# A mixture-of-experts layer whose expert blocks get fixed widths by rank of size, with weights loaded in 512 KB pieces

## What is computed

```python
logits = xf @ router_w
probs = jax.nn.softmax(logits, axis=-1)
topw, topi = jax.lax.top_k(probs, K)                    # K = 2 of E = 8 experts
h = jax.nn.silu(jnp.einsum('nd,edf->nef', xf, w1))      # w1: 8 x 1024 x 1024
ye = jnp.einsum('nef,efd->ned', h, w2)                  # w2: 8 x 1024 x 1024
routed = jnp.einsum('ne,ned->nd', combine, ye)
shared = jax.nn.silu(gate) * up @ shared_down
shared = jax.nn.sigmoid(xf @ shared_gate_w) * shared
return (routed + shared).reshape(b, t, d)
```

## Time and profile before

| | us |
|---|---|
| median of 3 executions | 1111.06 (1108.30 to 1111.72) |
| profiled execution, first to last instruction | 1107.2 |
| TensorE busy with matmuls | 1091.6 |
| DVE busy | 640.2 |
| ACT busy | 482.5 |
| POOL busy | 68.5 |
| share of 16 DMA engines, weights' queue | 33.4% |

### The profile page before, as it was taken

How to read it: one execution, slowest core, us unless ns; L and a number is a source line. 1 busy time by engine, 2 the same in 40 slices (tenths; PEclk the granted TensorE clock), 3 DMA queues, 4 the chain that set the end, 5 groups by cost and what they waited for, 6 DMA issues and landing times.

```text
span 1107.2 us, 16462 instructions
## 1 busy us (share of the span) xinstructions
PE 1091.6 (99%) x6240; PEld 949.3 (86%) x6240; DVE 640.2 (58%) x883; ACT 482.5 (44%) x713; POOL 68.5 (6%) x88
## 2 busy tenths in 40 slices
PE   7999999999999999999999999999999999999998
PEld 5889998787788999878789999898888988988877
DVE  6789967765666753343474423355655646555546
ACT  4503344557786221301324222245655646556540
POOL 2000000000000000000000530200000000000003
PEclk9999999999999999999999999999999999999999
DMA  7222201213322203622004442567577585666648
GB/s 251 76 77 77 76 11 67 76 58 124 104 77 77 71 13 126 207 77 76 1 1 170 152 111 77 169 256 254 190 255 261 184 292 205 241 234 226 235 153 283
DMA packets 76188, 157.02 MB, mean 142 GB/s; under 512 B 7130, under 2 KB 7628, under 8 KB 76131
## 3 DMA queue, kind: packets, MB, share of 16 engines
q1 hardware_dynamic: 64600, 127.30, 33.4%
q10 hardware_dynamic: 7306, 15.41, 3.8%
q0 software_dynamic: 4224, 13.55, 3.8%
HBM read 135.69 MB, written 20.54 MB: 141 GB/s over the span
## 4 chain that ended last, share of the span: by engine, by line
PE 89%; DVE 3%; ACT 2%; DMA 2%; DVEq 1%; issue 1%; POOL 1%; POOLq 0%; SPq 0%; ACTq 0%
PE ps L1725 21%; PE ps L1727 21%; PE ps L1726 21%; PE ps L2146 10%; PE ps L2147 5%; PE ps L1817 1%; PE ps L1764 1%; PE ps L2049 1%; PE ps L2050 1%; PE ps L1980 1%; PE ps L1981 1%; PE ps L1831 1%; DMA y_second<-expert_rows,slots 1%; ACT src_oh L808 1%; ACT w_hi L694 1%
## 5 line engine op out<-in xcount | busy, mean ns | idle before, releaser
L1025 DVE TENSOR_TENSOR w_lo<-w_raw,w_hi 128x2048 fp32r<-128x2048 f32 x107 | 242.3, 2290 | 135.7 <-ACT w_hi L694 133.4
L694 ACT CAST w_hi<-w_raw 128x2048 fp32r<-128x2048 f32 x107 | 201.5, 1911 | 86.4 <-PE ps L2050 36.2
L2146 PE MATMUL ps<-xe,w_hi 128*128 128x448 f32 x512 | 160.9, 375 | 0.0
L2147 PE MATMUL ps<-xe,w_lo 128*128 128x224 f32 x512 | 134.8, 263 | 0.0
L2146 PEld LDWEIGHTS ps<-xe,w_hi 128*128 128x128 f32 x512 | 95.9, 187 | 7.9
L1725 PE MATMUL ps<-w_hi,he_hi 128*128 128x512 f32 (+1 forms) x256 | 101.2, 395 | 0.0
L1727 PE MATMUL ps<-w_hi,he_lo 128*128 128x512 f32 (+1 forms) x256 | 100.2, 391 | 0.0
L1726 PE MATMUL ps<-w_lo,he_hi 128*128 128x512 f32 (+1 forms) x256 | 100.0, 391 | 0.0
L1725 PE MATMUL ps<-w_hi,xt_hi 128*128 128x512 f32 (+1 forms) x240 | 96.0, 400 | 4.0 <-DVEq L1334 2.0
L2147 PEld LDWEIGHTS ps<-xe,w_lo 128*128 128x128 f32 x512 | 97.5, 190 | 0.4
L1727 PE MATMUL ps<-w_hi,xt_lo 128*128 128x512 f32 (+1 forms) x240 | 93.7, 390 | 0.0
(11 more groups left out here) (330 smaller groups left out, 2001.0 us busy)
## 6 DMA issues: line engine op xcount, KB each, us to landing
w_raw<-in_L_ffn_w SPq DMA_DIRECT2D x64, 1024.0 KB, 5.6
w_raw<-in_L_gnn_W_neigh SPq DMA_DIRECT2D x8, 1024.0 KB, 5.5
w_raw<-in_L_gnn_W_self SPq DMA_DIRECT2D x8, 1024.0 KB, 5.1
w_raw<-in_L_ffn_shared_gate_up SPq DMA_DIRECT2D x8, 1024.0 KB, 6.3
w_raw<-in_L_mix_Wv SPq DMA_DIRECT2D x4, 1024.0 KB, 5.7
w_raw<-in_L_mix_Wk SPq DMA_DIRECT2D x4, 1024.0 KB, 5.0
w_raw<-in_L_mix_Wq SPq DMA_DIRECT2D x4, 1024.0 KB, 4.9
w_raw<-in_L_mix_Wo SPq DMA_DIRECT2D x4, 1024.0 KB, 5.0
```

What stands on the lines that cost most here:

```text
L694: copy(w_hi[b][:, s * HK:(s + 1) * HK, :], w_raw[s][:, :, :]).then_inc(hi_done, 1)
L1025: V_.tensor_tensor(w_lo[b][:, k, :], w_raw[s][:, :, :], as32(w_hi[b][:, k, :]), ALU.subtract).then_inc(lo_done, 1)
L2146: mat(PS(key)[:, a, 0:2 * B], wh[:, k, w_cols], xe[:, :, k, 0:B], start=k == 0, stop=False)
L2147: last = mat(PS(key)[:, a, 0:B], wl[:, k, w_cols], xe_hi[:, k, 0:B], start=False, stop=k == KF - 1)
```

## The change

- The experts are ranked by their number of rows on the chip (some 20 more small DVE instructions in the routing stage). Seven blocks have a fixed width (`CAPS`): ranks 2 and 3 get 208 rows, ranks 4 to 6 get 152, ranks 7 and 8 get 128. They are written out, not looped, in the order of ranks 2, 8, 3, 7, 4, 5, 6 (`ORDER` counts from rank 2 as 1), that is 208, 128, 208, 128, 152, 152, 152. A block of 128 has a single row tile; one of 152 has tiles of 128 and 24, one of 208 of 128 and 80.
- The loop of 224-row blocks stays behind them. It serves the largest expert (rank 1) and the rows of any expert that pass its fixed width. With the counts above no expert passes its width (203 and 201 of 208; 149, 147, 145 of 152; 121 and 71 of 128), and the loop runs once.
- Weights of the experts come in four pieces of 512 KB for each job (`PARTS`). SP reloads, ACT casts, DVE subtracts and TensorE waits piece by piece (`weights_in`).
- The zeros for all slots behind the fixed ones, 2016 rows or 8.3 MB, are written by POOL's queue at the start of the kernel from `ctx_s`, in 16 transfers; the zeros ahead of the loop (5.5 MB) are gone.
- POOL reads the token numbers of the twelve fixed tiles into `cols_f` with twelve transfers besides the two for the loop, all ahead of the first gather.

```diff
-    MAXB = X + (2 * N - X) // B + 1
-    SLOTS = MAXB * B
-    SLOTC = SLOTS // 112
-    assert SLOTC * 112 == SLOTS
+    CAPS = (208, 208, 152, 152, 152, 128, 128)
+    ORDER = (1, 7, 2, 6, 3, 4, 5)
+    FIXED = len(ORDER)
+    assert sorted(ORDER) == list(range(1, X)) and len(CAPS) == FIXED and max(CAPS) <= B
+    CAP = [CAPS[r - 1] for r in ORDER]
+    ROWS_OF = [(128, c - 128) if c > 128 else (c,) for c in CAP] + [BROWS]
+    TILE_AT = [sum(len(rows) for rows in ROWS_OF[:q]) for q in range(FIXED + 1)]
+    FIRST_ROW = [sum(CAP[:q]) for q in range(FIXED + 1)]
+    STATIC = FIRST_ROW[FIXED]
+    by_cap = sorted(CAPS)
+    MAXB = 1 + max(m + (2 * N - sum(by_cap[:m - 1]) - m) // B for m in range(1, X + 1))
+    SLOTS = STATIC + MAXB * B
+    SLOTC = -(-SLOTS // 112)
...
-    units += [("sd", 0, 0)] + [("xe", s, f) for s in range(BC) for f in range(2)]
+    xe_units = lambda q: [("xe", q, s, f) for s in range(len(ROWS_OF[q])) for f in range(2)]
+    y_units = lambda q: [("y", q, h, s) for h in range(2) for s in range(len(ROWS_OF[q]))]
+    he_units = lambda q: [("he", q, n) for n in range(KF // 2)]
+    units += [("sd", 0, 0)] + xe_units(0)
     units += [("sd", 0, i) for i in range(1, NT)]
+    for q in range(FIXED):
+        units += he_units(q) + xe_units(q + 1)[:2] + y_units(q)[:1] + xe_units(q + 1)[2:] + y_units(q)[1:]
     U0 = len(units)
...
+    PARTS = 4
...
+            every = sp.value_load(table[0:1, 1, 1:2], min_val=X, max_val=FIXED + MAXB - 1)
+            sp.wait_ge(lo_done, count_at(J_D, 1))
+            with sp.Fori(0, every) as j:
                 expert = sp.value_load(table[0:1, 0, bass.ds(j, 1)], min_val=0, max_val=X - 1)
                 for i in range(4):
                 for i in range(4):
-                    for s in range(2):
-                        sp.wait_ge(lo_done, j * 8 + (2 * (J_X + i - 1) + s + 1))
-                        view = (w1v if i < 2 else w2v)[:, bass.ds(expert, 1), s * HK:(s + 1) * HK,
+                    for s in range(PARTS):
+                        sp.wait_ge(lo_done, j * (4 * PARTS) + (count_at(J_X + i, s) - PARTS))
+                        view = (w1v if i < 2 else w2v)[:, bass.ds(expert, 1), s * PK:(s + 1) * PK,
                                                        (i % 2) * HW:(i % 2 + 1) * HW]
-                        sp.dma_start(w_raw[s][:, :, :], view.rearrange("p e k n -> p (e k) n")).then_inc(w_loaded[s], 16)
...
+            pool.wait_ge(pads_set, 1)
+            for r, count in ZEROED:
+                pool.dma_start(y_d[r:r + count, :], ctx_s[0:count, :, :].rearrange("p n t -> p (n t)")).then_inc(y_zeroed, 16)
...
+            for q in range(FIXED):
+                for s, rows in enumerate(ROWS_OF[q]):
+                    t, r = TILE_AT[q] + s, FIRST_ROW[q] + s * 128
+                    pool.dma_start(cols_f[0:rows, t:t + 1], slot_d[r:r + rows, :]).then_inc(cols_loaded, 16)
...
-            pool.wait_ge(ready[slot(("up", KF - 1))], use(("up", KF - 1)) + 1)
-            pool.wait_ge(prod_done, KF)
-            nc.gpsimd.memset(zrow[:, :], 0.0)
...
+            for q in range(1, FIXED):
+                pool.wait_ge(lo_out, rows_in[q - 1])
+                gather_rows(q)
...
+                if job >= J_X:
+                    for s in range(PARTS):
+                        act.wait_ge(part_loaded[s], by(16 * (job - J_X + 1), base, 64))
+                        copy(w_hi[b][:, s * PK:(s + 1) * PK, :], raw_part(s)).then_inc(hi_done, 1)
+                    return
...
+            def expert(q, j=None):
+
+                job, width = J_X + 4 * q, sum(ROWS_OF[q])
+                for h in range(2):
+                    split_hi(job + h + 1, j)
+                    for n in range(h * HK // 2, (h + 1) * HK // 2):
+                        key = ("he", q, n)
+                        in_s = he_s[:, n % 2, :, 0:width]
+                        wait_unit(key, j)
+                        copy(in_s, PS(key)[:, :, width:2 * width]).then_inc(he_copied, 1)
+                        act.wait_ge(he_added, by(q * (KF // 2) + n + 1, j, KF // 2))
+                        nc.scalar.activation(in_s, in_s, ACT.Silu).then_inc(silu_done, 1)
+                        act.wait_ge(silu_done, by(q * (KF // 2) + n + 1, j, KF // 2))
+                        copy(he_hi[:, 2 * n:2 * n + 2, 0:width], in_s).then_inc(hi_out, 1)
...
+            for q in range(FIXED):
+                expert(q)
...
-            act.wait_ge(zrow_set, 1)
-            for s in range(BC):
-
-                act.dma_start(y_b[block_rows(s), MAXB - 1, 0:HW], zrow[0:BROWS[s], 0:HW]).then_inc(y_stored[s], 16)
-                act.dma_start(y_b[block_rows(s), MAXB - 1, HW:D], zrow[0:BROWS[s], HW:D]).then_inc(y_rows, 16)
-            with act.Fori(blocks, MAXB - 1) as j:
-                for s in range(BC):
-                    act.dma_start(y_block(j, s, 0, D), zrow[0:BROWS[s], :]).then_inc(y_rows, 16)
...
+            dve.wait_ge(y_zeroed, 16 * len(ZEROED))
...
+            V_.scalar_tensor_tensor(size_key[:, :], cnt, float(X), iota_m8[:, :], ALU.mult, ALU.subtract)
+            V_.drain()
+            V_.tensor_tensor(larger[:, :, :], inner(size_key[:, :]), outer(size_key[:, :]), ALU.is_gt)
+            V_.drain()
+            V_.reduce_sum(size_rank[:, :], larger[:, :, :], axis=AX.X)
+            V_.drain()
...
+            def weights_in(job, k, base=None):
+
+                if k % PK == 0:
+                    pe.wait_ge(lo_done, by(count_at(job, k // PK), base, 4 * PARTS))
...
+                                if n == h * HK // 2 and a == 0:
+                                    weights_in(job + h, k, j)
+                                mat(PS(key)[:, a, 0:2 * width], wh[:, k, w_cols], xe[:, :, k, 0:width], start=k == 0, stop=False)
+                                last = mat(PS(key)[:, a, 0:width], wl[:, k, w_cols], xe_hi[:, k, 0:width], start=False,
+                                           stop=k == KF - 1)
...
+            for q in range(FIXED):
+                expert(q)
```

More of the change, by code:

```diff
@@ L618, in _ @@
             nc.gpsimd.memset(lg[:, NT - 1, :], 0.0)
+            for q in range(X):
+                nc.gpsimd.memset(iota_q[:, q:q + 1], float(ORDER[q] if q < FIXED else 0))
+                nc.gpsimd.memset(cap_q[:, q:q + 1], float(CAP[q] if q < FIXED else 0))
+                nc.gpsimd.memset(base_q[:, q:q + 1], float(FIRST_ROW[q] if q < FIXED else 0))
             nc.gpsimd.drain().then_inc(route_set, 1)
@@ L651, in _, with gather_rows @@
-            nc.gpsimd.drain().then_inc(zrow_set, 1)
-            with pool.Fori(0, blocks) as j:
-                pool.wait_ge(lo_out, j * BR + R0)
+            def gather_rows(q):
+                for s, rows in enumerate(ROWS_OF[q]):
+                    t = TILE_AT[q] + s
+                    nc.gpsimd.indirect_dma_start(
+                        out=xg[0:rows, s, :], out_offset=None, in_=xn2_d,
+                        in_offset=bass.IndirectOffsetOnAxis(ap=cols_f[0:rows, t:t + 1], axis=0)).then_inc(xg_loaded, 16)
@@ L2166, in _ @@
                         if h == s == 0:
-                            for rows in LATER:
-                                rows_across(*rows)
-            wh, wl = weights(J_X, blocks)
+                            for later in xe_units(q + 1)[2:]:
+                                rows_across(later, j)
+            for q in range(FIXED):
+                expert(q)
+            pe.wait_ge(table_ready, 1)
+            blocks = pe.value_load(table[0:1, 1, 0:1], min_val=1, max_val=MAXB - 1)
+            with pe.Fori(0, blocks) as j:
+                expert(LOOP, j)
```

311 lines of the change are left out of this document (184 added, 127 removed).

## The result

The changed kernel takes 1079.3 us (median of 4, 1077.7 to 1080.3) against 1111.0 for the kernel before (1108.3 to 1111.7): a ratio of 0.971, with a 95% interval from 0.967 to 0.975. It is faster by 31.6 us; the forecast was 1074, 37 faster. The two profiled executions are nearer to each other: 1107.2 and 1078.5 us from first to last instruction, 28.7 apart, and the forecast had 1107.2 and 1070.

The account below looks back on a forecast made before the run. TensorE was taken to bound the expert loop: eight blocks fall from 348.6 us to 287.7 of work plus 23 of weight waits, 310.7; with +0.5 at the start, -37.4, so 1111.1 becomes 1074 (own range 1066 to 1081).

Parts of the forecast that it names:

- TensorE's pairs: Expert loop: a pair of width w costs 0.033 + 3w/2400 us: 0.293 at 208, 0.223 at 152, 0.193 at 128.
- the bound that I set to nothing: Two weight loads a pair, at most 0.224 us, could add 2.0 us to a block of 128; taken as 0.
- The Trainium skill's rule that I set aside: A load of 128 columns takes 0.107 us, so no pair under 0.213; 1.3 us more for a block of 128.
- TensorE's y passes and transposes: Per block: y passes 21.8 us at 208 and 152, 10.9 at 128; transposes 1.4, 1.2 and 0.9.
- Waits inside a block: TensorE waits at Y0, 3.1 us in blocks of 128 and 1.5 at 152, none at 208; at Y1 0.5.
- the walk: Block of 128 followed through ACT and DVE: he 2's buffer is free at 16.2 us, TensorE there at 13.2.
- The inherited 2.9: The first block of 152 inherits the weights' delay: 1.7 us at H1, another 1.2 at Y0.
- H0 behind a block of 128: The next block's first pairs wait for late weights about 4 us: 3.8 before 208, 4.3 before 152.
- Start and tail: Early zeros delay the third weight piece at the kernel's start by 0.5 us (bound 0 to 4); the tail is unchanged.
- The rule against the change: Skill's advice to batch transfers to at least 1 MiB; if expert weight pieces did not overlap, 1223 us; chance 0.01.
- Weights fully hidden: Rival: the expert loop never waits for weights, as ACT and DVE work under 26 of 42 us; 1051 us, chance 0.13.
- Weights later: Rival: bursts at 320 GB/s, gathers and stores in the way, or the start's 4 us; 1082 to 1086, chance 0.20.

## Why the prediction was right, and where its steps were off

The direction, the main places and the order of size were right: 1079.3 against 1074, inside the forecast's own range. That it came so near is in part luck: terms of +10.7 and -11.8 cancel, and one of +5.9 was missing. It is also nearer by medians than by spans: of the forecast's 37.4 the medians gave 31.6 and the profiled executions 28.7, and the terms below belong to the latter. The terms, each as measured less forecast; waits are counted from start to start, as the forecast counted them, which is 0.1 to 0.3 us more than the idle time that a view gives:

- **TensorE's pairs.** The fixed part of a pair holds, the bound that I set to nothing does not. The forecast charged a pair by columns, 0.223 at 152 and 0.193 at 128. Measured over 64 pairs: 15.97 and 14.75 us, 0.250 and 0.230 a pair. The wide matmul of 304 columns is 0.143 by the forecast's own model; the narrow one behind it then takes 0.107 (an estimate, as the trace gives the sum alone), and the pair takes as much when it is cut to 64 columns. The earlier trace rows had shown 0.112 for matmuls that each load weights, and I used it as a bound on the sum of two (0.224) instead of on the narrow one alone. The term was too small by 1.7 us in each block of 152, 2.4 in each of 128 and 0.4 in each of 208: **+10.7**. The Trainium skill's rule that I set aside (LDWEIGHTS, columns over 1.2 GHz, 0.107 for 128) gives this very figure; the trace agrees at full clock, once it is applied to each matmul and not to the pair. At the 1.2 GHz level the trace gives 0.213, twice as much. And it is so for these float32 weights: matmuls of 196 bf16 columns earlier in the kernel, each with 128 columns of bf16 weights of its own, stand 0.088 apart, under 0.107 (20 of them in 1.93 us, the last one 0.25):

```profile
86.07 1.93 PE L1941 MATMUL ps<-by_column,by_place 128*128 128x196 bf16 x20
```

- **TensorE's y passes and transposes.** 23.6 us in a block of 152 (39.55 - 15.97) where I had 23.0, and 0.7 to 0.9 more in one of 128; eight transposes of 24 rows cost 0.5 rather than 0.3. +0.6 to 0.9 in five blocks, -0.2 in two, **+2.7**.
- **Waits inside a block** (Y0, Y1, and H1's and Y0's inherited delay). Forecast 14.6, measured 1.05 + 0.4 + 1.35 = 2.8: **-11.8**. Yet the walk was right: it said that the buffer of he 2 comes free 16.3 into a block of 128, and the y pass began at 16.6 (784.47 - 767.86). But TensorE is there at 15.5 and not at 13.2, so it waits 1.1 and has spent the rest on pairs. The same with blocks of 152: at Y0 TensorE is 1.7 later than forecast, and the wait of 1.5 is gone in blocks 5 and 6. In block 7 it stayed (1.35), though the pairs are as long: there ACT waited 2.0 us for H1's pieces to land (1.4 + 0.2 + 0.4), which it did not in block 6, and he 2 was added 1.8 later. The inherited 2.9 and Y1's 0.5 did not come either. Two errors of opposite sign and in the main one cause, so that only their sum was right.
- **H0 behind a block of 128.** Forecast 3.8 and 4.3; measured 5.0 and 5.65 (idle times 0.6 + 2.1 + 0.5 + 0.8 = 4.0 and 0.8 + 2.05 + 0.1 + 1.6 = 4.6): **+2.5**. The place and the chain were right, and the last piece was ready 35.4 us after the start of the block of 128, where the working had 32.5.
- **The clock.** Not in the working at all, and the largest miss in what a reader could act on. A wait was charged at its length; behind it TensorE ran at 1.2 GHz for part of H0. The two stretches are 26.17 and 23.73 us, undisturbed ones 19.18 and 15.97. Of the 7.0 and 7.75 more, some 10.5 pairs at 0.26 more each and 14.4 at 0.217 make 2.7 and 3.1, and waits the rest (4.3 and 4.6): **+5.9**. Keeping TensorE busy took 5.4 to 6.1 off the two stretches, which agrees.
- **Start and tail.** Forecast +0.5 and 0. The first pair of the loop stands at 725.66, and at 725.99 before: nothing. The V weights landed in 13.1 us under the zeros, without a gap on TensorE.
- **The rule against the change** that I weighed and left: the run with 1 MB pieces is 30 us slower here. The mean rate is nearly the same (235 and 239 GB/s over block 2). A quarter of a job is there after 3.8 us as a median and 3.5 at best, where 1 MB took 5.7 and 4.9; that this, and not the finer casts and subtractions, is what matters is likely but was not separated.

The five sums give 10.0, which is the excess of the table of stretches (320.6 - 310.7 = 9.9). *Weights fully hidden* (1051) was wrong, and the order of ACT's queue, the reason given, is the smaller part of why: the waits at Y0 come to 2.8, against 10.65 at H0, 5.9 by the clock, and 13.4 in TensorE's own work. *Weights later* (1082 to 1086) is near in size. Its slow bursts are not what was seen, the burst ran at 382 to 387 GB/s; its gathers in the way are there, but as a part of the waits at H0.
